# A post-norm transformer block on one Trainium2 core: the 96 steps of its local layers written out in place of a loop, weights and rotary table loaded once per layer

## What is computed

```
x = layernorm(x + latent_attention(x))
y = x
for i in range(6):                                   # DEPTH
    s = shift_tokens(y)                              # half of the width comes from the token before
    q, k, v = split(s @ Wqkv[i])                     # 128 -> 3 x 1024, 16 heads of 64
    q, k = l2norm(q) * q_scale[i], l2norm(k) * k_scale[i]
    q, k = rotary(q), rotary_inverse_scale(k)        # tables depend on the token alone
    y = local_attention(q, k, v) @ Wo[i] + y         # windows of 32, each sees itself and the one before
    h = norm(shift_tokens(y)) * g[i] + b[i]
    a, gate = split(h @ W1[i] + b1[i])               # 128 -> 2 x 341
    y = (a * gelu(gate)) @ W2[i] + b2[i] + y
x = layernorm(x + y)
```

## Time and profile before

| what | value |
|---|---|
| runs, us | 4651.01 median of 3 (4648.67, 4651.01, 4669.51) |
| profiled execution, us | 4670.98 |
| its span, us | 4669.2 |
| mean granted TensorE clock in the span | 0.959 |
| instructions in the span | 162098 |
| moved by DMA | 258.77 MB, 55 GB/s on average |
| `v_back` copies | 96 x 768 KB and 192 x 128 KB: 1 MB per step |
| weight loads, each 24 or 25 times | w_qkv 1024 + 512 KB, w_o 512 KB, w_1 and w_2 341 + 128 + 42.5 KB, small 4.5 KB, qk_row 128 KB |

### The profile page before, as it was taken

How to read it: one execution, slowest core, us unless ns; L and a number is a source line. 1 busy time by engine, 2 the same in 40 slices (tenths; PEclk the granted TensorE clock), 3 DMA queues, 4 the chain that set the end, 5 groups by cost and what they waited for, 6 DMA issues and landing times. The chain is left out here.

```text
span 4669.2 us, 162098 instructions
## 1 busy us (share of the span) xinstructions
PE 4135.5 (89%) x67078; PEld 2766.5 (59%) x67078; DVE 2915.5 (62%) x4217; ACT 2616.0 (56%) x4417; POOL 2805.6 (60%) x3584
## 2 busy tenths in 40 slices
PE   5879788689999999999999999999999999999994
PEld 2434344346666666666666666666666666666663
DVE  5565656466666666666666666666666666666664
ACT  2545353446666656656656566566665656656552
POOL 0000000177777777777777777777777777777771
PEclk8989798889999999999999999999999999999997
DMA  0000000112222222222222223222222222222223
GB/s 28 3 15 2 15 2 15 41 39 65 65 70 74 58 68 67 72 55 67 66 70 64 56 68 79 62 59 70 68 72 55 65 66 70 64 56 67 70 64 81
DMA packets 284568, 258.77 MB, mean 55 GB/s; under 512 B 122871, under 2 KB 258508, under 8 KB 271148
## 3 DMA queue, kind: packets, MB, share of 16 engines
q1 hardware_dynamic: 283820, 248.14, 20.0%
HBM read 117.63 MB, written 29.77 MB: 32 GB/s over the span
## 5 line engine op out<-in xcount | busy, mean ns | idle before, releaser
L787 DVE TENSOR_TENSOR products<-bank_d,table 128x1024 f32<-128x1024 f32 x772 | 938.1, 1216 | 684.4 <-ACT sq L614 679.7
L910 POOL TENSOR_TENSOR products<-products 128x2048 f32<-128x2048 f32 x192 | 871.0, 4536 | 313.8 <-DVE products L787 313.8
L413 PE MATMUL bank_d<-w_qkv,xT 128*128 128x512 f32 x1544 | 807.5, 626 | 18.7 <-issue 13.0
L614 ACT ACTIVATE sq<-bank_d 128x512 f32<-128x512 f32 x772 | 468.0, 606 | 469.9 <-PE bank_d L413 457.4
L947 POOL TENSOR_TENSOR qk_rot<-products,rnorm 128x2048 f32<-128x2048 f32 x192 | 695.6, 3623 | 14.0 <-POOL rnorm L929 12.7
L785 DVE TENSOR_REDUCE ss<-sq 128x16 f32<-128x1024 f32 x386 | 468.8, 1214 | 229.3 <-ACT sq L614 229.3
L874 POOL MEMSET ident<- 128x128 f32 x1 | 0.2, 205 | 915.1 <-POOLq L1064 915.1
L954 POOL TENSOR_TENSOR prob<-prob,inv_sum 128x1024 f32<-128x1024 f32 x192 | 365.4, 1903 | 307.3 <-DVE inv_sum L767 307.3
L1491 DVE TENSOR_REDUCE part_max<-s_max 128x1 f32<-128x512 f32 (+3 forms) x768 | 399.5, 554 | 152.2 <-PE s_max L1240 101.3
L478 PE MATMUL scores<-kT,qT 64*32 64x64 f32 x24576 | 430.4, 218 | 24.4 <-issue 24.4
L413 PE MATMUL bank_a<-w_qkv,xT 128*128 128x512 f32 x768 | 403.1, 607 | 49.7 <-ACT gate L669 47.5
(11 more groups left out here) (168 smaller groups left out, 7581.9 us busy)
## 6 DMA issues: line engine op xcount, KB each, us to landing
v_back<-v SPq DMA_DIRECT2D x96, 768.0 KB, 5.4
w_qkv<-in_Wqkv_dram SPq DMA_DIRECT2D x25, 1024.0 KB, 5.1
v_back<-v SPq DMA_DIRECT2D x192, 128.0 KB, 5.7
w_qkv<-in_Wqkv_dram SPq DMA_DIRECT2D x25, 512.0 KB, 5.4
xs<-x_layers SPq DMA_DIRECT2D x194, 64.0 KB, 2.1
w_o<-in_Wo_dram SPq DMA_DIRECT2D x24, 512.0 KB, 6.9
xr<-x_layers SPq DMA_DIRECT2D x96, 128.0 KB, 3.0
x<-x SPq DMA_DIRECT2D x96, 128.0 KB, 1.8
```

Source lines behind the costliest of these rows:

```text
L413: nc.tensor.matmul(bank[:, :], xT[:, P * a:P * (a + 1)], w_qkv[:, col:col + 512], start=True, stop=True).then_inc(d_filled if i < 8 else a ...
L614: nc.scalar.activation(sq[j % 2][:, 8 * c:8 * c + 8, :], bank_d[slot][:, :].rearrange("p (h d) -> p h d", d=DH), ACT.Square).then_inc(squa ...
L787: nc.vector.tensor_tensor(products[:, a, head:head + 8, :, :].rearrange("p h r (o d) -> p h r o d", o=2), bank[:, :].rearrange("p (h r d) ...
L910: link(nc.gpsimd.tensor_tensor(products[:, a, :, 0, :], products[:, a, :, 0, :], products[:, a, :, 1, :], ALU.add))
```

## The change

The loop goes: `rounds` writes all six layers out, and a step knows its layer and batch element as whole numbers. Every wait is on a constant. The waits and loads of the weights stand in the first batch element's steps alone (w_qkv for the next layer in the last one's), the table is made in the last batch element's steps, and the counts follow. The work of the engines on data is the same, apart from the loads and the table products that are no longer repeated.

```diff
         def rounds(eng, step_fn, last_fn=None):
-            for b in range(BATCH):
-                for p in range(POS):
-                    step_fn(Step(b, p))
-            with nc.Fori(1, DEPTH, engines=[eng.engine], hint_back_edge=True) as layer:
+            for layer in range(DEPTH):
                 for b in range(BATCH):
                     for p in range(POS):
-                        step_fn(Step(BATCH * layer + b, p))
+                        step_fn(Step(layer, b, p))
...
-                if runs(now) and s.p == 0:
-                    sp.wait_ge(table_ready, POS * (s.f + 1))
-                    load_qk_rows(s.f + 1)
-                if runs(now) and s.p == POS - 1:
+                if runs(now) and s.b == 0 and s.p == 0:
+                    sp.wait_ge(table_ready, POS * (s.layer + 1))
+                    load_qk_rows((s.layer + 1) % DEPTH)
+                if runs(now) and s.b == BATCH - 1 and s.p == POS - 1:
                     sp.wait_ge(d_filled, chunk_at(now, 7)[1] + 1)
-                    load_w_qkv(s.f + 1, 0, 2 * INNER, wqk_in)
+                    load_w_qkv((s.layer + 1) % DEPTH, 0, 2 * INNER, wqk_in)
...
-                if runs(back2) and s.p == 1 and in_rounds(s):
-
-                    load_wo(s.f)
+                if runs(back2) and s.b == 0 and s.p == 1 and in_rounds(s):
+
+                    load_wo(s.layer)
...
-                    if s.p == 2 and in_rounds(s):
-
-                        load_ffn(s.f)
+                    if s.b == 0 and s.p == 2 and in_rounds(s):
+
+                        load_ffn(s.layer)
...
-                    if s.p == POS - 1:
-                        pe.wait_ge(wqk_in, 16 * (s.f + 2))
+                    if s.b == BATCH - 1 and s.p == POS - 1:
+                        pe.wait_ge(wqk_in, 16 * (s.layer + 2))
                     pe.wait_ge(a_free, ring_a.at(s, "xT")[1] + 1)
-                if i == 8 and s.p == 0:
-                    pe.wait_ge(wv_in, 16 * (s.f + 1))
+                if i == 8 and s.b == 0 and s.p == 0:
+                    pe.wait_ge(wv_in, 16 * (s.layer + 1))
...
-                if s.p == 2:
-                    pe.wait_ge(wo_in, 16 * (s.f + 1))
+                if s.b == 0 and s.p == 2 and in_rounds(s):
+                    pe.wait_ge(wo_in, 16 * (s.layer + 1))
...
-                    if s.p == 3:
-                        pe.wait_ge(wffn_in, 64 * (s.f + 1))
+                    if s.b == 0 and s.p == 3:
+                        pe.wait_ge(wffn_in, 64 * (s.layer + 1))
...
-                    dve.wait_ge(table_ready, pair.n + 1)
+                    dve.wait_ge(table_ready, POS * pair.layer + pair.p + 1)
...
-                    make_table(s.f + 1, s.p)
+                    if s.b == BATCH - 1:
+                        make_table(s.layer + 1, s.p)
```

More of the change, by code:

```diff
@@ L55, in names_of_step @@
     def names_of_step(self, t):
-        return [n for n, _ in self.stage_names] if isinstance(t, int) and MAX_LAG <= t < PAIRS else self.names(t)
+        return self.names(t)
     def last_in_bank(self, step, name):
@@ L87, in before @@
             return sum(len(self.names(s)) for s in range(-1, t))
-        if isinstance(t, int) and t > PAIRS:
+        if isinstance(t, int) and t >= PAIRS:
             return self.before(t - 1) + len(self.names(t - 1))
@@ L101, with __init__ @@
 class Step:
-    def __init__(self, f, p):
-        self.f, self.p = f, p
-        self.t = POS * f + p
+    def __init__(self, layer, b, p):
+        self.layer, self.b, self.p = layer, b, p
+        self.f = BATCH * layer + b
+        self.t = POS * self.f + p
     def pair(self, lag):
@@ L119, in __init__ @@
         self.f = step.f + q // POS
+        self.layer = step.layer + (step.b + q // POS) // BATCH
         self.n = step.t - lag
@@ L238, in rounds @@
         def rounds(eng, step_fn, last_fn=None):
-            for b in range(BATCH):
-                for p in range(POS):
-                    step_fn(Step(b, p))
-            with nc.Fori(1, DEPTH, engines=[eng.engine], hint_back_edge=True) as layer:
+            for layer in range(DEPTH):
                 for b in range(BATCH):
                     for p in range(POS):
-                        step_fn(Step(BATCH * layer + b, p))
+                        step_fn(Step(layer, b, p))
             for t in range(PAIRS, PAIRS + MAX_LAG):
-                step_fn(Step(ROUNDS, t - PAIRS))
+                step_fn(Step(DEPTH, 0, t - PAIRS))
         def prev(s):
-            return Step(s.f, s.p - 1) if s.p else Step(s.f - 1, POS - 1)
+            if s.p:
+                return Step(s.layer, s.b, s.p - 1)
+            return Step(s.layer, s.b - 1, POS - 1) if s.b else Step(s.layer - 1, BATCH - 1, POS - 1)
         def chunk_at(pair, i):
@@ L278, in _, with load_w_qkv, load_qk_rows, load_wo @@
         def _(sp):
[L279 to L280 removed]
+            def load_w_qkv(layer, lo, hi, done):
+                sp.dma_start(w_qkv[:, lo:hi], w["Wqkv"][bass.ds(layer, 1), :, lo:hi]
                              .rearrange("one k n -> (one k) n")).then_inc(done, 16)
[L283 to L284 removed]
+            def load_qk_rows(layer):
+                sp.dma_start(qk_row[:, :, :], w["qk_rows"][bass.ds(layer, 1), :]
                              .rearrange("one (r d) -> one r d", d=DH).to_broadcast([P, 4, DH])).then_inc(qkrow_in, 16)
[L287 to L288 removed]
+            def load_wo(layer):
+                sp.dma_start(w_o[:, :, :], w["Wo"][bass.ds(layer, 1), :, :]
                              .rearrange("one (c k) n -> k (one c) n", k=P)).then_inc(wo_in, 16)
[L291 to L292 removed]
+            def load_ffn(layer):
+                layer = bass.ds(layer, 1)
                 sp.dma_start(w_1[:, :], w["W1"][layer, :, :].rearrange("one k n -> (one k) n")).then_inc(wffn_in, 16)
@@ L363, in step @@
                     sp.dma_start(dst[0:q, 0, :], old[P - q:P, 1, :]).then_inc(done, 16)
-                    if s.p == POS - 1:
-                        load_w_qkv(s.f + 1, 2 * INNER, 3 * INNER, wv_in)
+                    if s.b == BATCH - 1 and s.p == POS - 1:
+                        load_w_qkv((s.layer + 1) % DEPTH, 2 * INNER, 3 * INNER, wv_in)
                 if runs(back3):
@@ L686, in step @@
                 if runs(back3):
-                    if s.p == 3:
-                        act.wait_ge(wffn_in, 64 * (s.f + 1))
+                    if s.b == 0 and s.p == 3:
+                        act.wait_ge(wffn_in, 64 * (s.layer + 1))
                     bank = filled(s, "xn")
@@ L829, in step @@
                 if runs(back3):
-                    if s.p == 3:
-                        dve.wait_ge(wffn_in, 64 * (s.f + 1))
+                    if s.b == 0 and s.p == 3:
+                        dve.wait_ge(wffn_in, 64 * (s.layer + 1))
                     hidden_units(s, "A")
@@ L892, in _, with make_table @@
             pool.wait_ge(constants_ready, INIT)
-            def make_table(f, p):
-                pool.wait_ge(qkrow_in, 16 * (f + 1))
+            def make_table(layer, p):
+                pool.wait_ge(qkrow_in, 16 * (layer + 1))
                 rows = slice(2 * p, 2 * p + 2)
```

16 lines of the change are left out of this document (7 added, 9 removed).

## The result

The changed kernel takes **4795.99 us** (median of 4 runs, 4782.92 to 4812.6). The kernel of before, beside it, takes 4649.84 (4 runs, 4647.36 to 4669.51). The ratio is 1.0295, 95% interval 1.0273 to 1.0316: **slower by 3%**, where 4567 had been forecast, 2% faster. The profiled execution is one of 4812.6 us, of before 4671.0, 142 us more.

A forecast was written before the change was run, and what follows sets the result against it. TensorE's pace was taken to bound the local layers, with stops at ends of 256-instruction blocks. 4671.0 - 103 - 5 + 14 = 4577; between that and 4557 for run scatter, 4567 us was forecast, range 4540 to 4612.

The forecast's parts named there:

- The drift: In TensorE's written-out steps, removed weight waits move block ends 14 instructions, 7 matmuls, later per layer: matmul 569 to about 604.
- 103 + 5 us: Savings: 103.0 us from 80 loop steps written out at the 36.70 floor, 5 from stops in twelve already written-out steps.
- What stays: Stops left at block ends after the change: 8 us with w_o loads, 6 with v_back alone; +14, ends 0 and 50.
- I take 6: Last layer, block ends at matmul 597 to 604 beside v_back copies alone: 6 us, bounds 0 and 34.
- At 569 to 592 it cost nothing in 20 steps: A step's last block end at these matmuls was read as free of stops, from 20 steps of the profile before.
- these start up to 0.5 us sooner, which nobody waits for: On SP's queue, v_back and y2 start sooner once w_o loads ahead of them go; counted as no time.
- the stop at 1518.9 us: TensorE stop beside v_back copies without a w_o load, once in nine written-out steps of other positions, about 2 us.
- rival 3: Block ends stay put at matmul 617, 4.8 us a step for the last 30 steps: slower, 4711 us; chance 0.04.
- stops every step in the last layer: Sign that the forecast is wrong and rival 3 holds: TensorE stopping in each step of the last layer.

The follow-up runs named there:

- shift128: The changed kernel with 64 small matmuls (128 instructions) ahead of TensorE's first step: 4571.74 us, ratio 0.9808.
- late_v: The changed kernel with the v_back copies issued later, once the step's last attention output is copied out: 4562.65 us, ratio 0.9792.
- loop_once: The kernel of before with its loop kept, but weights and table made once per layer: 4675.15 us, ratio 1.0026.
- late_shift128: The changed kernel with v_back copies issued later and 64 small matmuls ahead of TensorE's first step: 4555.80 us, ratio 0.9778.
- shift32: The changed kernel with 16 small matmuls (32 instructions) ahead of TensorE's first step: 4681.53 us, ratio 1.0049.

## Why the prediction was wrong

**Right.** TensorE's pace bounds the layers, at a floor of 36.7 us a step. Blocks of 256 instructions are what the long steps come from, with the copies of v_back beside them (shift128 shows the one, late_v the other). The drift is 14 instructions per layer, counted before the run, and block ends in written-out code stay put. The bytes, 208.3 MB for "some 209". The fewer loads and table products are worth nothing by themselves (loop_once). What the sum took away, 103 + 5 us, is there to be had: late_shift128 loses nothing against the floor, and its 2.2% are 103 us (108 between the medians of that comparison), where the sum took away 108 and gave 14 back.

**The step that failed is "What stays"**, the term for v_back alone: "I take 6", with bounds 0 and 34. Measured: 240 us lost from step 4 on, nearly all of it in 70 steps of 3.4 us each: 15 us in the five steps with a w_o load, for which 8 were taken, and 225 in the others, for which the 6 stood. Three things were wrong in it.

1. *The bound was read from rows of another kind of step.* "At 569 to 592 it cost nothing in 20 steps": they were looped steps. In the loop SyncE has register operations of its own, and the timing differs. The kernel of before issues v_back there mostly 1.16 to 1.28 us behind the xT copy and never sooner, later still in many steps (up to 2.4, once 3.6); the changed one 0.97. SyncE's queue in a looped step, xT copy at 1818.24:

```profile
1818.39 0.88 SPq L349 DMA_DIRECT2D xs<-x  x2
1819.40 0.56 SPq L361 DMA_DIRECT2D v_back<-v  x1
```

With the preceding block end at matmul 443, 459 or 464 the lags of the clean looped steps are at most 0.34, 0.47 and 0.53. The change brings matmul 442 to 0.57 and stops there. The prediction saw only the loads move ("these start up to 0.5 us sooner, which nobody waits for") and asked of them who waits for the data. The fetch of instructions was the one that was hurt.

2. *The cause was put one block too late.* I looked at the block end where TensorE stops (569 to 604). In the changed kernel what decides is the one before it (439 to 475), where the block is asked for, against the issue of the copies. With that the stop at 1518.9 us, which I shared out at 2 us in nine steps, would have been a sign of the edge close by, and the drift a sign of which way it goes.

3. *A place that costs is paid in every step.* I gave rival 3 the right mechanism but put its place at matmul 617 and made it hang on a drift of twice 14. Its 30 steps of 4.8 us (4711) became 70 of 3.4, and the chance of 0.04 took the range from 569 to 604 to be nearly free, as the term did.

The Trainium skill, Runtime: NRT & Kernel Launch, Instruction fetch mechanics, calls crossing a block "mostly hidden" and gives taken branches as what breaks the fetching ahead. Of some 460 block ends of TensorE from 1062 to 4684 us, in code without a branch, 71 show a stop, 136.1 us in all; most are hidden, then, but those that are not make the kernel 5% longer. As for its blocks of 256 instructions, every count agrees.

Of what would show the prediction wrong, "stops every step in the last layer" came true, from the second layer on.

## What to carry to other kernels

Where TensorE runs many small matmuls, count its instructions between idle moments under "issue"; if the counts are multiples of 256, set the block ends before them against the issues of large DMAs. Written-out code fixes that phase for the whole program, for good or ill (4572 or 4828 us here with the same steps), so bound it by every place that a block end could take and by written-out rows alone, and move the DMA, or send it in pieces, rather than trust the place. And an instruction that is taken out, a wait or a register operation, shifts everything behind it: "costs nothing" has to include what comes to lie on what.

## What the runs showed of the hardware that was not expected

- With its block end from 0.5 us ahead of the issue of 1 MB of copies to 0.45 us behind it, and between matmuls 358 and 486, a block arrives in time; from 0.75 to 1.1 us behind, its packet starts 2.4 to 4.4 us later (median 3.4), about when the copies have drained. A quarter of a microsecond divides 0 stops of 147 from 20 of 24. Why it waits for nearly all of the copies stays open, and so does what tells the steps apart between 0.55 and 0.65, where 21 of 74 stop. The Trainium skill, DMA: Bandwidth & Descriptors, Arbitration, has each DMA engine take turns between its queues packet by packet, a packet being some 9 to 17 descriptors and at most 64. By that alone the fetch would wait for one packet of the copies. No run here shows how many of the profile's packets make one of those, so whether it explains the 3.62 us of step 40 stays open too.
- The packet's start is not the end of the wait: TensorE goes on some 2.5 us behind it (median 2.58 over 302 stops). In the 17 stops of shift32 with the packet 0.85 to 1.3 us behind the block end it went on 3.3 to 4.0 us behind that end. The 256 instructions of the densest stretches here, half of them matmuls of 32 or 64 columns, are through in 2.1 to 2.7 us.
- The stop itself is half of the price. 1.81 us idle in step 40 makes it 40.4 us in place of 36.7, since the granted clock is at 1.2 GHz for 3.4 us behind it.
- The block asked for at one block end is already needed at the next, 256 instructions on. In the 71 stops of the changed kernel TensorE never ran further than that on what it had.
